# A two-layer decoder kernel: second-layer projection weights prepared in the opening, blank pair rows written in layer 0, two turn banks and another order in layer 1

## What is computed

```
x += mamba(norm(x))                 # layer 0: state-space mixer, 8 heads
x += cross_attention(norm(x), ctx)  # 16 heads, rotary, biases
x += gated_recurrence(norm(x))      # c = f*c + i*g over the 64 tiles
x += grouped_attention(norm(x))     # layer 1: 16 query heads, 4 kv heads, rms norm inside
x += single_head_attention(norm(x), ctx)
x += mixture_of_experts(norm(x))    # 8 experts, top 2, and a shared expert
```

## Time and profile before

| | |
|---|---|
| median of 3 runs | 3503.76 us (3502.93 to 3503.86) |
| profiled execution | 3505.98 us, span 3504.2 us |
| busy share of the span | PE 89%, PEld 76%, DVE 79%, ACT 65%, POOL 44% |
| opening (`start`) | 0 to 87.8 us |
| `layer0` | 87.8 to 1885.6 us |
| `between` | 1885.6 to 1902.1 us |
| `layer1` | 1902.1 to 2988.2 us |
| `route` and `experts` | 2988.2 to 3504.2 us |

### The profile page before, as it was taken

How to read it: one execution, slowest core, us unless ns; L and a number is a source line. 1 busy time by engine, 2 the same in 40 slices (tenths; PEclk the granted TensorE clock), 3 DMA queues, 4 the chain that set the end, 5 groups by cost and what they waited for, 6 DMA issues and landing times. The chain is left out here.

```text
span 3504.2 us, 95628 instructions
## 1 busy us (share of the span) xinstructions
PE 3118.5 (89%) x27092; PEld 2676.8 (76%) x27093; DVE 2768.9 (79%) x8748; ACT 2282.2 (65%) x8269; POOL 1530.3 (44%) x5116
## 2 busy tenths in 40 slices
PE   6699999999999999999985788888888888499998
PEld 4578888888888888888874677777777777287998
DVE  5588888888888888888872677777777786587776
ACT  3367777777777777777762677777777776133333
POOL 1244455444445444454441355554555454033333
PEclk8699999999999999999996899999999999599999
DMA  5000001001000100000003500000000000122443
GB/s 166 25 31 27 27 28 34 27 27 33 30 27 27 36 27 27 30 33 27 27 24 123 201 15 18 15 18 15 15 18 15 18 15 11 47 89 112 137 137 91
DMA packets 92030, 162.12 MB, mean 46 GB/s; under 512 B 13379, under 2 KB 57584, under 8 KB 91952
## 3 DMA queue, kind: packets, MB, share of 16 engines
q1 hardware_dynamic: 73744, 102.32, 9.7%
q0 software_dynamic: 18208, 58.84, 4.7%
HBM read 102.85 MB, written 61.79 MB: 47 GB/s over the span
## 5 line engine op out<-in xcount | busy, mean ns | idle before, releaser
L385 POOL TENSOR_TENSOR tiny<-tiny 128x1 f32<-128x1 f32 x3456 | 780.3, 226 | 844.4 <-DVE tiny L372 604.0
L726 ACT ACTIVATE work<-bank,att 128x128 f32<-128x128 f32 x2048 | 722.2, 379 | 90.3 <-DVE att L716 84.8
L726 ACT ACTIVATION_READ_ACCUMULATOR work<-bank,att 128x1 f32 x2048 | 447.2, 218 | 0.0
L716 DVE TENSOR_REDUCE att<-bank 128x4 f32<-128x512 f32 x512 | 335.0, 686 | 141.2 <-PE bank L709 139.1
L208 PE MATMUL bank<-work,w0p 128*128 128x128 f32 x3072 | 428.1, 279 | 3.5 <-ACT r_tfi_ L1092 1.8
L208 PEld LDWEIGHTS bank<-work,w0p 128*128 128x128 f32 x3072 | 383.6, 194 | 12.3 <-ACT work L1017 2.6
L188 PE MATMUL bank<-w1r,workr 128*128 (+3 forms) x1058 | 361.0, 341 | 17.1 <-DVE workr L1793 16.6
L745 PE MATMUL bank<-const,work 128*128 128x128 f32 x2048 | 318.1, 278 | 52.5 <-ACT work L751 35.4
L1191 DVE SCALAR_TENSOR_TENSOR work<-work,small 128x127 f32<-128x127 f32 (+2 forms) x1152 | 319.8, 346 | 14.2 <-ACT work L1031 9.5
L190 PE MATMUL bank<-w1r,workr 128*128 (+3 forms) x1058 | 323.0, 305 | 0.0
L189 PE MATMUL bank<-w1r,workr 128*128 (+3 forms) x1058 | 322.5, 305 | 0.0
(11 more groups left out here) (331 smaller groups left out, 7671.0 us busy)
## 6 DMA issues: line engine op xcount, KB each, us to landing
work<-decay_sums SPq DMA_DIRECT2D x64, 512.0 KB, 3.6
pair_rows<-work POOLq DMA_DIRECT2D x4, 5934.0 KB, 45.1
work<-pair_rows SPq DMA_DIRECT2D x91, 258.0 KB
work<-in_ctx SPq DMA_DIRECT2D x128, 128.0 KB, 2.1
x_res<-in_x POOLq DMA_DIRECT2D x8, 1024.0 KB, 17.0
recurrence_out<-r_xo_ SPq DMA_DIRECT2D x64, 128.0 KB, 1.7
work<-recurrence_out SPq DMA_DIRECT2D x64, 128.0 KB, 2.0
out_dram<-work POOLq DMA_INDIRECT x91
```

Of the source, the lines that this page charges most:

```text
L385: e.tensor_tensor(out_, a_, b_, ALU.add if b_ is three_halves else ALU.mult)\
L716: e.tensor_reduce(a_nm[:, 4 * g:4 * g + 4], sc_banks[g % 2][:, :].rearrange("p (h k) -> p h k", k=P), AX.X, ALU.max, negate=True).then_inc ...
L726: last = e.activation(Pb[g % 2][:, c * P:c * P + P], sc_banks[g % 2][:, c * P:c * P + P], ACT.Exp, bias=a_nm[:, 4 * g + c:4 * g + c + 1], ...
```

## The change

1. The phase `between` is gone. The eight transpose jobs become jobs 32 to 39 of `start`, which now has 42 jobs with `out_proj` last; SP loads the raw grouped-attention weights and the small vectors in `start`, after its 32nd job; splitting them and the transpose of the gate weights go to `start` too. The running-sum matrix products are moved ahead of the last ten jobs on TensorE, and the corresponding instructions on ScalarE and VectorE too. The second-layer weights have buffers of their own (`w1p`, `w_s`), and a part of the experts' weights (`w_dnp`) is placed in one of them later.
2. The computing of `v_row` and the load of one bias row (`dbv_row`) go to the head of `layer1`.
3. The blank rows are written in `layer0`, by GpSimd, before its first tile. The row in SBUF has 260 numbers in place of 516, and each quarter of the rows is written by three transfers (256, 256 and 4 numbers of each row): 12 transfers in place of 4, 35,328 row pieces in place of 11,776.
4. The grouped attention has two turn banks (4 and 7). Even groups use bank 4, odd ones bank 7, and `turn(g)` waits for the take of group g - 2. The routing piece `g_` moves from bank 7 to bank 5, which it shares with `d_`.
5. The order in `layer1` is another. In TensorE's loop, from one `scores(0)` to the next, with t the tile of the turns:
   - before: scores 0, d_values, d_project, turn 0, scores 1, s_transpose, turn 1, s_out, s_project, turn 2, g_logits, turn 3, d_scores, g_transpose, values, turn_inverse, d_turn, s_turn_qk, d_transpose
   - after: scores 0, d_values, d_project, turn 0, scores 1, s_transpose, s_out, turn 1, s_project, turn 2, g_transpose, turn 3, d_scores, values, g_logits, s_turn_qk, d_turn, turn_inverse, d_transpose

   VectorE, from the maxima of groups 0 and 1:
   - before: max 0 1, g_norm, d_residual, lo s_o, normed s, s_head, max 2 3, lo s, take 1, s_residual, g_logits, inverse, take 3, s_rotary, d_maximum, s_join, normed d, normalise
   - after: max 0 1, d_residual, normed s, s_head, lo s_o, max 2 3, lo s, take 1, s_residual, take 3, d_maximum, g_norm, s_rotary, inverse, g_logits, normed d, s_join, normalise

   ScalarE, from the exponents of groups 0 and 1:
   - before: exp 0 1, d_heads, take 0, copy s_tr, exp 2 3, take 2, tanh, copy d_v, d_exp, s_values, take_inverse, copy d_pt, s_heads, copy g_tr, copy d_tr, copy s_o
   - after: exp 0 1, d_heads, take 0, copy d_v, copy s_tr, exp 2 3, take 2, copy g_tr, s_values, tanh, d_exp, s_heads, copy d_pt, take_inverse, copy d_tr, copy s_o

   GpSimd keeps the order s, g, d of its three `newton`, but `add_bias` of a tile now stands directly behind `newton d` of the same tile and so waits for VectorE's `normed d`.

```diff
...
 
                 jobs0 += [(wx[r * P:(r + 1) * P, :], D, plain(w_rx, g * D + r * P), 1.0, None),
                           (wu[r * P:(r + 1) * P, :], D, plain(w_ru, g * D + r * P), 0.5, None)]
+        for r in range(2):
+            jobs0 += [(uo[r * P:(r + 1) * P, :], D, plain(w_uo, r * P), 0.5, None),
+                      (d_Wq[r * P:(r + 1) * P, :], D, plain(w_dq, r * P), 1.0, None),
+                      (d_Wk[r * P:(r + 1) * P, :], D, plain(w_dk, r * P), 1.0, None),
+                      (d_Wv[r * P:(r + 1) * P, :], D, plain(w_dv, r * P), 1.0, None)]
         jobs0 += [(out_proj[r * P:(r + 1) * P, :], DI, to(w_out, r * P), 1.0, nw_row) for r in range(2)]
         w0 = weights("w0", stage0, jobs0)
...
             def _(e):
                 e.dma_start(const[:, :], table[:, 0:C_END]).then_inc(S["const_loaded"], 16)
                 e.dma_start(dt_stage, in_proj[DI + XBC:DI + XBC + NH, :]).then_inc(S["dt_loaded"], 16)
-                w0[0](e)
+                w0[0](e, range(PAIRS_OF_X))
+                for dst, src in ((qkv_raw[:, :, 0:D], s_wq.rearrange("(k p) n -> p k n", p=P)),
+                                 (qkv_raw[:, :, D:D + KV * DH], s_wk.rearrange("(k p) n -> p k n", p=P)),
+                                 (qkv_raw[:, :, D + KV * DH:NQ], s_wv.rearrange("(k p) n -> p k n", p=P)),
+                                 (so_raw, s_wo.rearrange("(k p) n -> p k n", p=P)),
+                                 (gcol, s_g.rearrange("(j p) -> p j", p=P)),
+                                 (dbq, d_bq.rearrange("(j p) -> p j", p=P)),
+                                 (dbk, d_bk.rearrange("(j p) -> p j", p=P)),
+                                 (lbb, lb_bias.partition_broadcast(P)),
+                                 (gate_stage, gate_w)):
+                    with nc.allow_non_contiguous_dma(reason="small vectors, once"):
+                        e.dma_start(dst, src).then_inc(S["l1_small"], 16)
+                w0[0](e, range(PAIRS_OF_X, len(jobs0)))
                 e.wait_ge(S["p_kept"], 1)
                 e.dma_start(cum_dram.rearrange("(k c) (h t) -> (c h) k t", k=NT // P, h=NH),
...
+                    last = e.matmul(bank[6][:, k:k + P], pdt[3][:, k:k + P], upper, start=True, stop=True)
+                last.then_inc(S["p_cumT"], 1)
                 w0[1](e, range(PAIRS_OF_X, len(jobs0)))
 
+                e.wait_ge(S["l1_small"], 9 * 16)
+                for c in range(2):
+                    last = e.transpose(small_bank[:, 2 * NH + c * E:2 * NH + c * E + E], gate_stage[:, c * P:c * P + P],
+                                       ident[0:E, 0:E])
+                last.then_inc(S["q_gate"], 1)
                 e.wait_ge(S["bv_lo"], 1)
+                e.wait_ge(S["b_gate"], 1)
...
                 e.activation(expA, expA, ACT.Exp).then_inc(S["expA_ready"], 1)
                 e.wait_ge(S["p_min"], 1)
                 e.activation(pdt[1], pdt[1], ACT.Exp).then_inc(S["p_chain"], 1)
                 e.wait_ge(S["p_chain"], 1)
                 e.activation(pdt[3], pdt[1], ACT.Ln, bias=const[:, C_ONE:C_ONE + 1]).then_inc(S["p_act"], 1)
+                w0[2](e, range(PAIRS_OF_X, len(jobs0)))
+                e.wait_ge(S["q_gate"], 1)
+                e.activation(w_gate[:, :, :], small_bank[:, 2 * NH:2 * NH + 2 * E].rearrange("p (k n) -> p k n", k=2),
+                             ACT.Copy).then_inc(S["b_gate"], 1)
+                e.wait_ge(S["l1_wg"], 1)
+                e.activation(w_sqkv[:, 0], qkv_raw, ACT.Copy).then_inc(S["l1_whi"], 1)
+                e.activation(w_so[:, 0], so_raw, ACT.Copy).then_inc(S["l1_whi"], 1)
                 e.wait_ge(S["p_cumT"], 1)
                 e.activation(cumT, bank[6][:, :], ACT.Copy).then_inc(S["p_kept"], 1)
...
-                w0[3](e, range(PAIRS_OF_X, len(jobs0)))
+                e.wait_ge(S["l1_small"], 9 * 16)
+                for k in range(2):
+                    e.tensor_tensor(so_raw[:, k, k * P:k * P + P], so_raw[:, k, k * P:k * P + P], ident, ALU.add)
+                for k in range(2):
+                    last = e.tensor_scalar(qkv_raw[:, k, :], qkv_raw[:, k, :], gcol[:, k:k + 1], None, ALU.mult)
+                last.then_inc(S["l1_wg"], 1)
 
                 e.wait_ge(S["expA_ready"], 1)
...
+                w0[3](e, range(PAIRS_OF_X, len(jobs0)))
+                e.wait_ge(S["l1_whi"], 2)
+                e.tensor_tensor(w_sqkv[:, 1], qkv_raw, w_sqkv[:, 0].bitcast(F32), ALU.subtract)
+                e.tensor_tensor(w_so[:, 1], so_raw, w_so[:, 0].bitcast(F32), ALU.subtract).then_inc(S["l1_wlo"], 1)
                 e.wait_ge(S["bo2_mm"], 1)
                 e.tensor_tensor(bo2_row, small_bank[:, D:2 * D], bo2_in, ALU.add).then_inc(S["bias_rows_ready"], 1)
...
+        slots = nc.dram_tensor("pair_rows", (BLANKS * P, ROW), F32, kind="Internal").ap()
+        blank = wk(D + 4)
         def head_cols(blk, odd, g):
 
             return blk * NH + 2 * g + odd
 
...
+            two = len(pt_banks) == 2
+            pt_bank = pt_banks[0]
+            def taken(e, b, g):
+                if two:
+                    n = 2 * b + g // 2
+                    if past(n): e.wait_ge(S[pre + ("_ptv" if g % 2 else "_pt")], n)
+                elif past(4 * b + g):
+                    e.wait_ge(S[pre + "_pt"], 4 * b + g)
+            def all_taken(e, b):
+                if two:
+                    e.wait_ge(S[pre + "_pt"], 2 * b + 2)
+                    e.wait_ge(S[pre + "_ptv"], 2 * b + 2)
+                else:
+                    e.wait_ge(S[pre + "_pt"], 4 * b + 4)
 
             def scores(e, b, pair):
...
-                if past(4 * b + g): e.wait_ge(S[pre + "_pt"], 4 * b + g)
+                taken(e, b, g)
                 for h in range(4):
-                    last = e.transpose(pt_bank[:, h * P:h * P + P], Pb[g % 2][:, h * P:h * P + P], ident)
+                    last = e.transpose(pt_banks[g % len(pt_banks)][:, h * P:h * P + P], Pb[g % 2][:, h * P:h * P + P], ident)
                 last.then_inc(S[pre + "_ptr"], 1)
 
...
 
             def turn_inverse(e, b):
                 e.wait_ge(S[pre + "_rinv"], b + 1)
-                e.wait_ge(S[pre + "_pt"], 4 * b + 4)
+                taken(e, b, 4)
                 for blk in range(2):
                     last = e.transpose(pt_bank[:, blk * P:blk * P + P], a_wide[:, blk * P:blk * P + P], ident)
...
             def values(e, b):
-                e.wait_ge(S[pre + "_pt"], 4 * b + 4)
+                all_taken(e, b)
                 e.wait_ge(S[pre + "_v"], b + 1)
...
-                               [bank[3], bank[4]], bank[5], bank[6], "c_x2")
+                               [bank[3], bank[4]], [bank[5]], bank[6], "c_x2")
 
         with phase("layer0") as block:
...
 
             @block.gpsimd
             def _(e):
+                e.memset(blank, 0.0).then_inc(S["blank_ready"], 1)
+                e.wait_ge(S["blank_ready"], 1)
+                e.iota(blank[:, D + 2:D + 3].bitcast(I32), [[0, 1]], base=TOKENS, channel_multiplier=1)\
+                    .then_inc(S["blank_ready"], 1)
+                e.wait_ge(S["blank_ready"], 2)
+                for k in range(4):
+                    rows_k = slots.rearrange("(s k p) d -> k p s d", k=4, p=P)[k]
+                    for at, n, of in ((0, D, 0), (D, D, 0), (2 * D, 4, D)):
+                        e.dma_start(rows_k[:, :, at:at + n], blank[:, of:of + n].unsqueeze(1).to_broadcast([P, BLANKS // 4, n]))\
+                            .then_inc(S["blank"], 16)
                 def scale_tokens(b):
                     x3 = m_xt_.rearrange("p (h d) -> p h d", d=HD)
...
-                               s_P, s_PT, s_rT_, [bank[2], bank[3]], bank[4], bank[1], "s_x4")
-        slots = nc.dram_tensor("pair_rows", (BLANKS * P, ROW), F32, kind="Internal").ap()
-        wpos[0] = WORK - ROW
-        blank = wk(ROW).unsqueeze(1)
+                               s_P, s_PT, s_rT_, [bank[2], bank[3]], [bank[4], bank[7]], bank[1], "s_x4")
 
         with phase("layer1") as block:
             @block.sync
...
+                project32(e, bank[5][:, 0:D], d_state[:, :, :], w_uo, 2, 0, D).then_inc(S["b_v"], 1)
                 def s_transpose(b):
                     e.wait_ge(S["s_xn"], b + 1)
...
                         src = (d_xn_ if c < 2 else d_ctx_)[:, (c % 2) * P:(c % 2) * P + P]
...
                     e.wait_ge(S["g_xn"], b + 1)
                     if past(b): e.wait_ge(S["g_lg"], b)
+                    e.wait_ge(S["d_qk_sb"], min(b + 3, NB) if isinstance(b, int) else b + 3)
                     for c in range(2):
-                        last = e.transpose(bank[7][:, c * P:c * P + P], g_xn_[:, c * P:c * P + P], ident)
+                        last = e.transpose(bank[5][:, c * P:c * P + P], g_xn_[:, c * P:c * P + P], ident)
                     last.then_inc(S["g_tr"], 1)
 
                 def g_logits(b):
                     e.wait_ge(S["g_xnT"], b + 1)
                     for c in range(2):
```

(16 more changed lines are left out.)

271 lines of the change are left out of this document (104 added, 167 removed).

## The result

The changed kernel takes 3533.89 us (median of 4 runs, 3528.94 to 3538.86) against 3503.74 us of the kernel before on the same chip: ratio 1.0084, 95% interval 1.0068 to 1.0100. It is slower by 30 us where the forecast was 3444 us and 60 us faster.

What follows compares the result with a forecast made beforehand. Layer 1, the largest phase, was taken as bound by a loop of waits, no engine full. Terms -51 - 16.5 + 1.0 - 2.4 + 5.4 - 8.0 + 11.4 = -60.1 gave a 3444 us median, range 3422 to 3480.

Steps and rivals of the forecast that it cites:

- part 4: Blank rows moved to layer 0: layer 1 stall gone, -8.0 us; late running-sum loads in early tiles, +11.4 us.
- Rival 3: Start of layer 0: GpSimd held by its own issues to about 225 us, kernel slower at 3547 us; chance 0.07.
- opening: End of the opening: ten more jobs delay the copy of the running sums, +5.4 us, bounds 0 to 10.
- `between` gone: Between the layers: the whole phase from SP's first load to its first of layer 1 goes, -16.5 us.
- v_row and GpSimd's issues, fill of layer 1: Start of layer 1: v_row, an addition and a bias load add 1.0 us; GpSimd's four issues leaving saves 2.4.
- recurrence load stall: Layer 1: VectorE's wait for a 128 KB load beside the blank-row writing goes, -8.0 us.
- period of layer 1 and the rest of its tiles: Layer 1 loop: period from 16.03 to 15.1 us over 55 tiles, -51 us; kept range 14.7 to 15.6.
- tail of layer 1, `route`, `experts`: End of the kernel: routing and experts keep their instructions; no term in the sum.
- decay_sums loads late: Early tiles of layer 0: three running-sum loads each 5.7 us late, two thirds coming through, +11.4 us, bounds 0 to 29.
- rival 1: Layer 1: another wait, s_values ahead of tanh and d_exp on ScalarE, makes the period 15.6, time 3471 us; chance 0.19.
- The walk: One layer 1 period in the new order with old spacings: two paths end together at 15.0 us, 15.1 taken.
- The sizes inside the writing: Blank-row writing in layer 0: 1 KB pieces 65 us, 16-byte pieces 32 us, the middle of nothing to 65.

Runs made afterwards that it cites:

- experiments 5: Changed kernel with its twelve blank-row transfers issued three at a time behind scale_tokens of tiles 0 to 3, instead of all ahead of the loop: 3499.40 us.
- experiment 6: Changed kernel with its twelve blank-row transfers in groups of five, five and two, behind scale_tokens of tiles 0, 2 and 4: 3466.93 us.
- experiment 2: Changed kernel with blank rows still written in layer 0, but as four whole-row transfers instead of twelve, c_o_ moved to the shared work buffer: 3449.00 us.
- experiment 9: Changed kernel with blank rows as three whole-row transfers behind rotate of tiles 0 to 2, between the loads, c_o_ in the shared work buffer: 3449.35 us.

## Why the prediction was wrong

**The step that failed** is in part 4: "12 issues at 6.01 / 4 = 1.5 us hold GpSimd for 18 us". The price of an issue was right (7.61 + 7.40 + 2.96 = 18.0 us for the twelve), and the sum was made as if the queue took any number. It was wrong by 88 us of GpSimd and 84 of layer 0. Rival 3 named this mechanism and got 0.07, because "the present issues show no sign of a full queue". The four issues of the earlier trace rows showed that 11,776 rows fit and nothing of 35,328; absence of a sign in a third of the load was read as evidence. Its price came near: a hold to 225 us and 3547 were worked out, 198.6 and 3534 came. That it came near is in part luck, since the price rested on 5.5 ns for each piece and on a queue that lets GpSimd go when two thirds are written. Its limit (11,776 rows) was too low, and its picture, a queue that takes more as it drains, is not what experiments 5 and 6 show.

**The other terms**, against the stage table:

| term | forecast | measured |
|---|---|---|
| opening | +5.4 | +4.2 |
| `between` gone | -16.5 | -16.5 |
| v_row and GpSimd's issues, fill of layer 1 | +1.0 - 2.4 | -1.1 |
| recurrence load stall | -8.0 | -7.8 (third interval 23.03 to 15.24) |
| period of layer 1 and the rest of its tiles | -51 | -36 |
| tail of layer 1, `route`, `experts` | 0 | -3.6 |
| decay_sums loads late | +11.4 | +4 in twelve tiles (experiment 2), +21 (experiment 6) |

*Period.* The term of layer 1 was mis-sized: 15.38 came for 15.1, within the bounds, and half way to rival 1. The walk can be laid beside the timeline of the changed kernel, time zero at the maximum of 2411.84:

```profile
2411.84 1.29 DVE L789 TENSOR_REDUCE att<-bank 128x4 f32<-128x512 f32 x2 [0.39 <-PE bank L782]
...
2420.57 0.66 PE L818 MATMUL bank<-const,work 128*128 128x128 f32 x4
...
2421.26 0.69 DVE L829 COPY work<-bank 128x512 f32<-128x512 f32 x1 [0.33 <-PE bank L818]
...
2423.03 0.42 DVE L1842 TENSOR_TENSOR work<-bank,const 128x256 f32<-128x256 f32 x1
...
2423.75 0.22 ACT L1731 ACTIVATE work<-bank 128x64 f32<-128x64 f32 x1 [2.47 <-DVE work L1848]
...
2424.29 0.41 DVE L1835 TENSOR_SCALAR work<-x_res,tiny 128x256 f32 x1
2424.45 0.37 ACT L1753 ACTIVATE work<-bank,tiny 128x128 f32<-128x128 f32 x1
...
2425.35 0.60 PE L1611 MATMUL bank<-const,work 128*128 128x128 f32 x4
...
2426.04 1.16 PE L782 MATMUL bank<-work 32*128 32x128 f32 x16
```

Turn 3 stands at 8.73 (walk: 8.8), take 3 at 9.42 (9.46), rotary at 11.19 (10.99), s_values at 11.91 (11.71), d_exp at 12.61 (12.16), normed d at 12.45 (12.53), d_transpose at 13.51 (13.28), scores 0 at 14.20 (13.84). VectorE was free for the maximum at 14.99 (14.97), 0.39 before it could start. So VectorE's path was right, and the other is late: 0.20 at rotary, for which ScalarE waits 2.5 us, and 0.25 more through s_values and tanh ahead of d_exp. This is rival 1's mechanism. D_exp slips by 0.45, near its 0.5, but 0.22 of that is taken up again before d_transpose, and the period ends 0.28 above the forecast. Normed d did not wait for newton, where the walk had it wait.

*The other part of the miss in layer 1.* Three intervals are 18.2 us and not 15.38. Before, three were 17.2 and not 16.03. So 8.4 us beyond the period against 3.5, and 63 intervals x 0.65 = 41 us of gain come down to the 36 of the table. In one of them the clock is seen to fall (windows of the changed kernel):

```profile
2084.00:2099.00 15.00, 13.52 (x134) 11.20 (x131) 12.29 (x44) 11.26 (x51) 7.30 (x36) 1.00 0.06 18
2099.00:2103.00 4.00, 3.87 (x24) 3.31 (x25) 1.81 (x9) 2.43 (x8) 2.41 (x10) 0.52 0.15 36
2103.00:2107.00 4.00, 4.00 (x20) 3.79 (x21) 2.92 (x11) 3.06 (x17) 1.00 (x6) 0.63 0.10 30
2107.00:2111.00 4.00, 3.81 (x37) 3.17 (x35) 2.85 (x7) 3.25 (x14) 2.24 (x10) 1.00 0.00 0
```

At 1.00 ahead and behind, 0.52 and 0.63 in between, with TensorE almost without a pause (3.87 and 4.00 of 4). 0.5 is the 1.2 GHz level, which it has for most of those 8 us. Before the fall TensorE was busy 13.52 of 15 us. The other five long intervals have the same fall. Over 8 us the mean granted clock is 0.58 in each of the three of the changed kernel (2099, 2440 and 2842 us), and 0.79 in each of the three of the kernel before (2376, 2714 and 2892 us): the clock loses about twice as much now, and the interval is 2.8 us longer where it was 1.2. Why it falls, and why by more now, is not shown. The number of such intervals varies between kernels with the same layer 1: experiment 2 has one.

*Late loads.* The 10.3 us of experiment 2 from issue to use agree with the 11 assumed; 17.4 - 4.2 = 13 us of waiting gave only 4 to 5 us in the first twelve tiles, a third and not two thirds. For the form that was written (experiment 6), 35 us of waiting gave 21, near the two thirds. The sizes inside the writing were off both ways. From the first issue to the release four transfers of 1 KB pieces and one of 16 bytes took 146.81 - 92.80 = 54.0 us, the next three and two 195.66 - 146.81 = 48.9: that solves to 11.8 and 6.7 us each, 95 us for the eight of 1 KB (65 assumed) and 27 for the four of 16 bytes (32 assumed). These are estimates and rather high, since both stretches include the near-idle end of the hold; even so the 16-byte pieces were not at the dear end of the 0 to 65 us that the prediction allowed them.

*The rest of the sum.* Two kernels without the hold take 3448 and 3449 us, within 5 us of the forecast. That is in part luck, for errors cancel. By the traces of experiment 2 and of the kernel before, the tiles of layer 1 gain 41 us where 51 were forecast, layer 0 loses 6.7 where the late loads were to cost 11.4, and the end of the kernel, which was to stay, is 4.0 us shorter.

## What to carry to other kernels

Count the rows that an engine hands to its DMA queue in one go, not only the time per issue, and compare with the largest run that the trace shows passing: beyond it the price of the next issue is unknown and may be the whole transfer ahead of it. A long write on an engine that the first tile needs is worth whole rows and few transfers; a place between the loads of the first tiles took away the late loads (experiment 9), though no measurable time. When a profile shows nothing under a reason "issue", look at who issues what, and vary rows, transfers, bytes and spacing one at a time.
